# Which engine makes three of the products, and two small reorderings, in a fused state-space and mixture-of-experts kernel

## The reference

```python
x = L0_attn_x                                  # (8, 512, 256)
x = x + _layernorm(_L0_attn_ref(_layernorm(x), ...))
x = x + _layernorm(_L0_ffn_ref(_layernorm(x), ...))
```

```python
h = layernorm(x) * norm_w + norm_b
h = h @ in_proj_w.T
h = silu(causal convolution of h with 4 taps)
proj = h @ x_proj_w.T                          # dt_in (1), B (16), C (16)
dt = softplus(dt_in @ dt_proj_w.T + dt_proj_b)
state = exp(A * dt_t) * state + B_t * x_t      # over 512 time steps
y = einsum(state, C_t) + D * x_t
out = silu(y) @ out_proj_w.T + shortcut
```

## Time and profile before

| | us |
|---|---|
| median of 3 executions | 1394.33 |
| lowest and highest | 1393.41, 1395.83 |
| the profiled execution, its own time | 1393.79 |
| its span in the profile | 1392.0 |
| PE busy | 1194.2 |
| DVE busy | 1069.5 |
| POOL busy | 1045.7 |
| ACT busy | 796.5 |

### The profile page before, as it was taken

The page is one execution under the profiler, slowest core; times in us unless marked ns, Lnnn a source line. Parts: engine busy times, 40 slices in busy tenths (PEclk is TensorE's granted clock), DMA queues, the critical chain, the costliest instruction groups (busy, mean ns, idle before and its releaser), DMA issues.

```text
span 1392.0 us, 15477 instructions
## 1 busy us (share of the span) xinstructions
PE 1194.2 (86%) x4894; PEld 535.3 (38%) x4895; DVE 1069.5 (77%) x1409; ACT 796.5 (57%) x1386; POOL 1045.7 (75%) x558
## 2 busy tenths in 40 slices
PE   5668978887996996997798798898999999999995
PEld 2222223222332432432332243243545656656663
DVE  4588899999999999899999998799241116677675
ACT  5757679779778877877967875736431111111111
POOL 0579999999999999899999999989033723554453
PEclk9889999999999999999999999999999999999998
DMA  3921210330340141042034015001278522222220
GB/s 109 277 69 60 94 61 1 122 138 0 103 157 0 63 152 46 14 140 106 1 108 137 0 63 207 20 1 55 82 270 291 180 64 73 86 79 79 84 63 15
DMA packets 72068, 127.67 MB, mean 92 GB/s; under 512 B 8759, under 2 KB 48448, under 8 KB 67904
## 3 DMA queue, kind: packets, MB, share of 16 engines
q1 hardware_dynamic: 60432, 103.72, 22.2%
q0 software_dynamic: 7152, 16.81, 3.8%
q10 hardware_dynamic: 4416, 6.29, 1.3%
HBM read 97.79 MB, written 31.76 MB: 93 GB/s over the span
## 4 chain that ended last, share of the span: by engine, by line
PE 59%; DVE 21%; ACT 12%; issue 5%; DMA 1%; DVEq 0%; POOLq 0%; POOL 0%; ACTq 0%; SPq 0%
DVE state L1126 11%; PE psX L1697 10%; PE psY L1574 10%; PE psX L1632 5%; PE bank L1531 5%; DVE bx L1114 5%; PE bank L1487 4%; ACT psX L793 3%; PE psY L1645 3%; PE bank L1714 2%; PE psY L1714 2%; PE bank L1469 2%; PE bank L1470 2%; PE bank L1471 2%; DMA xin<-in_x 1%
## 5 line engine op out<-in xcount | busy, mean ns | idle before, releaser
L517 POOL TENSOR_TENSOR state<-state,cbc 128x1024 f32<-128x1024 f32 x256 | 599.2, 2367 | 10.2 <-DVE state L1126 10.2
L1126 DVE TENSOR_TENSOR_SCAN state<-psX,bx 128x1024 f32<-128x1024 f32 x256 | 580.9, 2282 | 25.9 <-ACT psX L793 22.2
L793 ACT ACTIVATE psX<-dt,aneg 128x511 f32<-128x511 f32 x512 | 331.3, 680 | 166.4 <-DVE state L1126 166.0
L506 POOL TENSOR_TENSOR bx<-xh,bbc 128x1024 f32<-128x1024 f32 x120 | 284.8, 2374 | 89.3 <-DVE state L1126 47.1
L1574 PE MATMUL psY<-state,ident 64*64 64x512 f32 x2048 | 268.0, 617 | 0.0
L1531 PE MATMUL bank<-prow,ident 128*128 128x512 f32 x272 | 151.0, 638 | 59.4 <-DVE bx L1114 57.5
L1114 DVE TENSOR_TENSOR bx<-xh,bank 128x1024 f32<-128x1024 f32 x136 | 162.9, 1198 | 15.4 <-PE bank L1531 15.3
L998 ACT ACTIVATE sg<-psX 128x512 f32<-128x512 f32 x39 | 23.3, 597 | 196.6 <-PE psX L1697 191.4
L1574 PEld LDWEIGHTS psY<-state,ident 64*64 64x64 f32 x2048 | 61.9, 133 | 166.3 <-issue 118.4
L1531 PEld LDWEIGHTS bank<-prow,ident 128*128 128x128 f32 x272 | 44.7, 192 | 149.5 <-DVE bx L1114 107.8
L581 POOL DMA_INDIRECT ysl<-shared_rows,idx x39 | 40.3, 1034 | 80.7 <-DVE idx L1292 75.7
(11 more groups left out here) (212 smaller groups left out, 1798.2 us busy)
## 6 DMA issues: line engine op xcount, KB each, us to landing
cbc<-bc_rows SPq DMA_DIRECT2D x32, 1024.0 KB, 6.6
bbc<-bc_rows SPq DMA_DIRECT2D x16, 1024.0 KB, 6.4
slot_in<-ao SPq DMA_DIRECT2D x1, 5011.5 KB, 35.2
xsl<-slot_in SPq DMA_DIRECT2D x39, 128.5 KB
xin<-in_x SPq DMA_DIRECT2D x8, 512.0 KB, 4.1
xr<-in_x SPq DMA_DIRECT2D x8, 512.0 KB, 5.5
x_rows<-ao SPq DMA_DIRECT2D x8, 512.0 KB, 3.4
xn_rows<-xr SPq DMA_DIRECT2D x8, 512.0 KB, 3.2
```

Of the source, the lines that this page charges most:

```text
L506: nc.gpsimd.tensor_tensor(bx[q % RB][:], xh[par][:, h * CH:(h + 1) * CH], bbc[:, n // 2].unsqueeze(1).broadcast_to([P, CH, L]), ALU.mult). ...
L517: nc.gpsimd.tensor_tensor(w[:], w[:], cbc[:, n].unsqueeze(1).broadcast_to([P, CH, L]), ALU.mult).then_inc(weighted, 1)
L793: e = nc.scalar.activation(decay[q % RD][:, c, 1:L], dt[par][:, h * CH + c, 1:L], ACT.Exp, scale=aneg[:, h * CH + c, n:n + 1])
L1126: nc.vector.tensor_tensor_scan(st[q % RS][:].rearrange("p c t -> p (c t)"), decay[q % RD].rearrange("p c t -> p (c t)"), bx[q % RB][:].rea ...
```

## The change

There are three edits.

1. The table `BY_POOL`: DVE makes the injections of the steps 12 and 30, which POOL made, and POOL makes that of step 14, which DVE made. `spread_b` follows the table on PE.
2. On ACT, three of the four sums of squares of batch `i + 2` stand at step 20 instead of step 10.
3. On PE, the first of the four `loss` stands in step 18 behind the sums and ahead of the front's matmuls L1455, instead of at the start of step 19.

```diff
-    BY_POOL = [q % 2 == 0 and q not in (14,) for q in range(Q)]
+    BY_POOL = [q % 2 == 0 and q not in (12, 30) for q in range(Q)]
...
-                if q == 10:
+                if q == 20:
                     for j in range(1, J):
                         row_pass(J + j, ACT.Square, mv0[par][:, j, 0:1], mv0[par][:, j, 1:2])
...
                     if do_front and q in LOSS_AT:
-                        loss(i + 1, 1 - par, q)
+                        if q > LOSS_AT[0]:
+                            loss(i + 1, 1 - par, q)
                     elif not BY_POOL[(q + 2) % Q]:
...
                         total(i - 1, 1 - par, q + Q - SUM_LAG)
+                    if do_front and q == LOSS_AT[0] - 1:
+                        loss(i + 1, 1 - par, q + 1)
                     if do_front:
                         front(i + 1, 1 - par, q)
```

## The result

| | before | after |
|---|---|---|
| median, us | 1394.76 (4 executions, 1393.41 to 1395.83) | 1422.03 (4 executions, 1420.33 to 1422.72) |
| the profiled execution, its own time | 1393.79 | 1422.62 |
| its span | 1392.0 | 1420.8 |

The changed kernel is slower: ratio 1.0194, 95% interval 1.0177 to 1.0212, or +27.3 us where +21.4 had been summed up. The direction held; the sum was 6 us short.

The account below looks back on a forecast made before the run. The bound was taken to be a chain changing engine, DVE with ACT's decays and PE's spreads, POOL following. Terms 9.6 + 6.6 + 1.0 + 4.2 = 21.4 us on 1393.8 gave 1415 us, range 1400 to 1424.

Parts of the forecast that it names:

- Injections 12 and 14: Steps 12 to 14: scan 13 comes 2.6 us later through PE's queue, scan 14 gains 1.2; +9.6 us.
- PE stays fast: Around dtin: inserted spread and sums take up the slow stretch, dtin takes 3.7 us; 1401 us, chance 0.12.
- The first loss: Steps 18 to 20: projection ends later, ACT's square, minimum and spread 21 come 0.7 us later; +4.2 us.
- room to spare: First batch at the early loss: no output projection in PE's queue, so no delay was counted there.
- The squares: ACT, steps 10 to 20: moving three squares, some 1.7 us, costs zero, bounds -0.3 and +0.3 per batch.
- just reaches DVE's next free slot: ACT at step 20: normalisation behind the moved squares still comes in time for DVE, so zero cost.
- Injection 30: After scan 29: spread 30 lengthens PE's unbroken run by 0.95 us in seven batches; +6.6 us.
- The last batch: No dtin, ends in transposes: spread 30 and its injection cost between 0 and 2.5 us, taken as +1.0.
- ACT late: Softplus chain after dtin misses by 1.3 us in seven batches: 9 us more, 1424 us, chance 0.12.
- hidden: Scans have slack for the extra spreads, batches grow by 0.2 us or less: 1395 us, chance 0.08.
- POOL bound: POOL's queue of weighings and injections is the bound; one operation less per batch saves 19 us: 1375 us, chance 0.08.
- the first term: The sum's part for steps 12 to 14 around dtin: +1.4 us per batch in seven batches, +9.6 us.

Follow-up runs that it names:

- the combined version: Kernel before with all even injections on POOL, ACT's first square at step 18, half the output projection ahead of spread 17: 1383.21 us against 1395.60 (0.9910).
- all even: Kernel before with injection 14 on POOL too, so that POOL makes the injections of every even step: changed by -2.1 us (0.9991).

## Why the prediction was nearly right, step by step

- **Injections 12 and 14.** Predicted: dtin ends 2.88 us later, 0.3 of it hidden, 1.2 us gained at scan 14, +9.6 us in all. Measured: dtin ends 3.14 us later after scan 11 (4.80 to 7.94), 0.28 hidden, 1.23 gained, +11.2. The step held, in its mechanism and its slack. The low clock was assumed to be paid once in either order; it moved from dtin onto the inserted spread and sums, but with PE's pause 1.8 us longer it was 6.8 us long in all seven batches of the kernel after, 3.4 us in four of seven before. That it ran low in either order is shown; why it was the longer stretch each time isn't.
- **PE stays fast** (the rival) was half true. Dtin took 4.11 us on average and not the 5.74 of the sum, so the step that priced it with the mean of before was wrong by -1.6 us. But spread 12 and the sums took 3.81 (7.92 less 4.11) where they were priced at 1.97 at full clock, +1.8 us. The two errors cancel; the rival counted only the first.
- **The first loss.** Predicted 0.7 us in six batches and 0 in the first; measured 0.69 in six and 2.65 in the first. The failed step is "room to spare": without an output projection PE comes to the loss 1.80 us before its logarithm is ready. That was the cover that the prediction had counted at about 1 us for the later batches, and it was gone in the one batch that it had excluded.
- **The squares.** Predicted 0 (bounds 0.3); measured 0.24 in four batches, 0.66 in one, 1.6 us in all. With nothing moved but them, 1.9 us. The sentence that the normalisation "just reaches DVE's next free slot" was not a row, and was not so.
- **Injection 30.** Predicted 0.95 in seven batches, 6.6 us; measured 0.86 and 6.0. The last batch: predicted +1.0; it has +1.39 at scan 30 and -3.06 at scan 14, where injection 14 left DVE, and 1.6 us elsewhere in it and in the tail, -0.1 together. The -3.06 was missing: the last batch had been priced for injection 30 alone.
- **What was in no term.** A second stretch at half clock in the third batch (1.6 us), and 2 us at the start of the first scan and in the first batch. They are in no fixed relation to the edits: in the first batch, scan 5 to 6 moved by 0.85 us in the kernel after, -1.53 in the one with injection 12, +1.47 in the combined version.
- **ACT late and hidden**, the two other rivals. PE's matmuls waited for the logarithm once, 1.80 us in the first batch; in the others it was ready at least 0.76 us before the loss. And the spreads weren't hidden: the batches took 117.0 to 120.3 us where some 117 to 118 had been named as the sign, the first 126.2 (120.8 before).
- **POOL bound** fell: POOL's work shrank by 17.1 us and its waiting for scans grew from 10.2 to 47.8; with 18.4 us more work on POOL than before (all even), the time did not rise. The Trainium skill (Perfetto Trace Analysis, section "Identifying the Most-Contended Engine") would relieve the engine with the highest occupancy. Of the elementwise engines that is DVE (77%), with POOL (75%) close behind. Adding work to DVE did cost time, so the trace agrees in the direction for DVE, but not by way of DVE's own work, which cost nothing at injection 12, and taking work off POOL gained nothing: the shares didn't say who was waited for.

That the sum came as near as 6 us is in part luck. In the first term two errors cancel, -1.6 and +1.8 us a batch, and the 3.06 us that the last batch gained stand against 3.6 us that were in no term. What is left is mostly the first batch's loss (2.65), the squares (1.6) and the first term (1.6).

Open: the single edits sum to more than the whole. Injection 12 (+22.3), injection 30 (+10.6), the loss (+9.5) and the squares (+1.9), with 11.7 us off for scan 14 in eight batches, give 32.6 us, and the kernel after has 27.3. The loss and injection 30 are each 3 us above what their fixed places add up to. Their mean clock was lower in the slower executions, which points at more low stretches; that these are the cause isn't shown, since only one execution of each was traced.

## What to carry to other kernels

When a step is moved to another engine, count what it adds to every queue that feeds it: here one product on DVE brought a spread on PE, and this spread had to wait for a bank at the head of the queue, ahead of work that was ready. Before an idle time is called a gain, look at who is ready behind it: 0.97 us won at a minimum were taken back within two scans in five of seven batches. And price the first and the last batch apart, since the queue there lacks the work that covers a wait in the others.

## What the runs showed of the hardware

- In these runs the granted clock was worth time only where TensorE was waited for. Throw-away matmuls raised it from 0.963 to 0.978 and saved 14 us in the changed kernel; in the combined version they raised it from 0.967 to 0.975, and saved nothing between the scans around dtin. The Trainium skill (TensorE: Matmul & The Clock Gate, section "Why this matters for your kernels") advises against pauses of TensorE between bursts; by that rule both would gain, and the trace agrees for the clock but not for the time of the second.
- Taking a matmul away can slow the next ones: without spread 14 the output projection took 5.30 us, 3.4 of them at 1.2 GHz, instead of 3.62 at 2.4 GHz, behind a pause of 2.46 us. The length of the pause alone doesn't settle it. Behind 2.46 us it took 3.62 in the fourth batch of the same kernel; behind 2.12 us in the changed kernel it took 3.62 in five batches and 4.34 in the third.
- Some of the spread between executions of one kernel follows the mean clock: all even injections took 1385.7 us at 0.968 and 1393.2 to 1394.7 us at 0.962. At a fixed place, the distances between scans repeat to about 0.01 us (0.69 or 0.70 added at the first loss in all six later batches of the kernel with edit 3 alone).
